# Reordering the steps of a software-pipelined cross-attention on three engines

## The reference

```
q = LN(x) @ Wq + bq          # 32 x 128
k = ctx @ Wk + bk            # 257 x 128
v = ctx @ Wv + bv            # 257 x 128
p = softmax(mask(q k^T / sqrt(8)))   # per head, 32 x 257
x = x + concat(p v) @ Wo + bo
```

## Time and profile before

| | |
|---|---|
| runs | 2421.90, 2426.17, 2428.85 us; median 2426.17 |
| profiled execution: its own time | 2426.17 us |
| its span | 2424.0 us, 55879 instructions |
| TensorE, VectorE, ScalarE, GpSimd busy | 83%, 75%, 60%, 37% |

### The profile page before, as it was taken

The page is one execution under the profiler, slowest core; times in us unless marked ns, Lnnn a source line. Parts: engine busy times, 40 slices in busy tenths (PEclk is TensorE's granted clock), DMA queues, the critical chain, the costliest instruction groups (busy, mean ns, idle before and its releaser), DMA issues. The chain is left out here.

```text
span 2424.0 us, 55879 instructions
## 1 busy us (share of the span) xinstructions
PE 2014.7 (83%) x15622; PEld 1559.9 (64%) x15622; DVE 1811.6 (75%) x5679; ACT 1444.7 (60%) x3917; POOL 905.8 (37%) x1342
## 2 busy tenths in 40 slices
PE   3799999999999999994250168999999989859997
PEld 2588888888888888872140036777777756526665
DVE  5788888888888888864757646888888878754554
ACT  3455555555555555555254537888888878745443
POOL 2433333333333333321124503333333347534554
PEclk8799999999999999996575578999999999969999
DMA  4211111111111011100000012222222200010001
GB/s 134 63 32 31 30 30 30 30 30 30 30 30 28 23 27 28 30 3 1 0 0 0 0 30 65 69 65 66 69 69 68 58 2 1 1 26 1 1 0 35
DMA packets 113672, 77.03 MB, mean 32 GB/s; under 512 B 12384, under 2 KB 99776, under 8 KB 113472
## 3 DMA queue, kind: packets, MB, share of 16 engines
q1 hardware_dynamic: 112086, 73.99, 11.4%
q10 hardware_dynamic: 1194, 1.58, 0.2%
q0 software_dynamic: 320, 0.60, 0.1%
HBM read 71.67 MB, written 4.46 MB: 31 GB/s over the span
## 5 line engine op out<-in xcount | busy, mean ns | idle before, releaser
L758 ACT ACTIVATE a_prob<-a_neg,a_nmax 128x289 f32<-128x289 f32 x512 | 269.9, 529 | 173.7 <-DVE a_nmax L684 171.8
L650 POOL TENSOR_TENSOR a_xn<-a_z,g 128x256 f32<-128x256 f32 x128 | 93.1, 727 | 585.9 <-DVE a_z L714 585.9
L803 PE MATMUL a_score<-a_xnT,a_qT 128*128 128x290 f32 x1536 | 274.2, 314 | 33.7 <-DVE a_qT L738 32.8
L1639 ACT ACTIVATE b_prob<-b_neg,b_nmax 128x257 f32<-128x257 f32 x512 | 255.2, 500 | 70.7 <-DVE b_nmax L1586 70.6
L803 PEld LDWEIGHTS a_score<-a_xnT,a_qT 128*128 128x128 f32 x1536 | 215.6, 190 | 85.6 <-issue 76.9
L830 PE MATMUL a_out<-a_probT,a_xn 128*128 128x256 f32 x1024 | 269.5, 386 | 0.3 <-DVE a_probT L699 0.3
L729 DVE TENSOR_SCALAR a_prob<-a_prob,a_rinv 128x256 f32<-128x256 f32 x512 | 256.9, 561 | 4.5
L684 DVE CUSTOM_DVE_ANT_0 a_neg<-a_score,a_bias 128x289 f32<-128x289 f32 x512 | 216.7, 454 | 40.4 <-PE a_score L803 36.4
L1586 DVE CUSTOM_DVE_ANT_0 b_neg<-b_score,b_bias 128x257 f32<-128x257 f32 x512 | 195.9, 421 | 50.5 <-PE b_score L1682 48.1
L830 PEld LDWEIGHTS a_out<-a_probT,a_xn 128*128 128x128 f32 x1024 | 175.6, 190 | 20.8 <-DVE a_probT L699 2.3
L1560 POOL TENSOR_TENSOR b_last_part<-b_v_rows,b_prob 128x128 f32<-128x128 f32 x128 | 52.0, 406 | 317.4 <-ACT b_prob L1639 317.4
(11 more groups left out here) (472 smaller groups left out, 5273.5 us busy)
## 6 DMA issues: line engine op xcount, KB each, us to landing
a_raw<-in_ctx SPq DMA_DIRECT2D x128, 128.0 KB, 3.2
b_raw<-in_ctx SPq DMA_DIRECT2D x128, 128.0 KB, 3.2
a_kept<-keep SPq DMA_DIRECT2D x32, 257.0 KB, 3.8
b_kept<-keep SPq DMA_DIRECT2D x32, 257.0 KB, 3.6
b_v_rows<-ctx_tail_values SPq DMA_DIRECT2D x32, 256.0 KB, 3.5
a_tail<-latents_normalised SPq DMA_DIRECT2D x64, 64.0 KB
latents_normalised<-lat_affine SPq DMA_DIRECT2D x8, 256.0 KB, 2.3
out<-x SPq DMA_DIRECT2D x1, 2048.0 KB
```

What stands on the lines that cost most here:

```text
L758: nc.scalar.activation(prob[:, par, grp, :], neg[:, grp, :], ACT.Exp, bias=nmax[:, par, grp:grp + 1], scale=-1.0, accum_out=rsum[:, par, g ...
L803: last = nc.tensor.matmul(score_ps[grp % 2][:, 0:even(KEYS0)], qT[:, a, un, bn, 4 * grp:4 * grp + 4, :], xnT[:, c, n, :], start=(p == 0), ...
L1639: nc.scalar.activation(prob[:, n, grp, :], neg[:, par, grp, :], ACT.Exp, bias=nmax[:, par, grp:grp + 1], scale=-1.0, accum_out=rsum[:, n, ...
```

## The change

The lists of VectorE, ScalarE and TensorE in `xattn1` are put in another order. No instruction is added, removed or resized.

| engine | order in a step before | order in a step after |
|---|---|---|
| TensorE | turns(s), weight(s) and raw(s+4), score(s+2), k and v(s+3), projection, last_part(s), values(s) | score(s+2), turns(s), weight(s) and raw(s+4), projection, last_part(s), k and v(s+3), values(s) |
| VectorE | probT(s), reciprocal(s+1), once per tile: sum or x, masks 0 and 1(s+2), kT(s+3), masks 2 and 3(s+2), own(s) | mask 0(s+2), probT(s), masks 1 to 3(s+2), reciprocal(s+1), kT(s+3), own(s), once per tile: x or sum |
| ScalarE | probT(s), turned_in(s+4), exp 0 and 1(s+2), v(s+3), exp 2 and 3(s+2), oT | exp 0(s+2), probT(s), turned_in(s+4), exp 1 to 3(s+2), oT, v(s+3) |

The sum of a tile moves from the start of the next tile's first step to the end of its own last step, and the addition to `x` from the third step of the next tile to the end of its second; VectorE's tail is one step shorter. The wait of `own` for the sum goes, since the sum now stands ahead of it in the same list.

```diff
--- before.py
+++ after.py
@@ -1589,46 +1589,43 @@
 
                 def step(g, j):
                     s, t, u, b = g * 8 + j, tile_of(g, j), j // 4, j % 4
+                    if live(g, j, 2):
+                        mask(g, j, 0)
                     if live(g, j, 0):
                         dve.wait_ge(turned[0], s + 1)
                         nc.vector.tensor_copy(probT[:, 0, :], turn_ps[0][:]).then_inc(probT_ready[0], 1)
+                    if live(g, j, 2):
+                        for grp in range(1, GROUPS):
+                            mask(g, j, grp)
                     if live(g, j, 1):
                         n = (j + 1) % 4
                         dve.wait_ge(exped, s * 4 + 8)
                         wait(dve, weight_ready, s - 2)
                         nc.vector.reciprocal(rinv[:, n, :], rsum[:, n, :]).then_inc(rinv_ready, 1)
-                    if b == 0 and live(g, j, -1):
-                        dve.wait_ge(own_ready, s)
-                        wait(dve, oT_ready, t - 1)
-                        nc.vector.tensor_reduce(oT_sum[:], own[:].rearrange("p b h l -> p b l h"), AX.X, ALU.add).then_inc(sum_ready, 1)
-                    if b == 2 and live(g, j, -4):
+                    if live(g, j, 3):
+                        n = (j + 3) % 4
+                        dve.wait_ge(k_done, s + 4)
+                        dve.wait_ge(kept_loaded[(j + 3) // 4 % 2], (g + (j + 3) // 8 + 1) * 16)
+                        nc.vector.scalar_tensor_tensor(kT[:, n, :], turn_ps[0][:, 0:N_CTX], k.bk1, kept[:, (j + 3) // 4 % 2, n, :],
+                                                       ALU.add, ALU.mult).then_inc(k_ready, 1)
+                    if live(g, j, 0):
+                        dve.wait_ge(out_ready, s + 1)
+                        dve.wait_ge(in_copied, s + 5)
+                        nc.vector.tensor_tensor(own[:, b].rearrange("p h l -> p (h l)"), out_ps[:, 0:P], turned_in[:, (j + 4) % 8, W0:W0 + P],
+                                                ALU.mult).then_inc(own_ready, 1)
+                    if b == 1 and live(g, j, -4):
                         dve.wait_ge(biased, t)
                         dve.wait_ge(proj_ready, t)
                         xt = k.x[:, ds((t - 1) * D, D)]
                         nc.vector.tensor_tensor(xt, proj_ps, xt, ALU.add).then_inc(x_added, 1)
                         wait_apart(k, dve, x_added, t)
                         tile_stats(k, t - 1).then_inc(x_stats_ready, 1)
-                    if live(g, j, 2):
-                        mask(g, j, 0)
-                        mask(g, j, 1)
-                    if live(g, j, 3):
-                        n = (j + 3) % 4
-                        dve.wait_ge(k_done, s + 4)
-                        dve.wait_ge(kept_loaded[(j + 3) // 4 % 2], (g + (j + 3) // 8 + 1) * 16)
-                        nc.vector.scalar_tensor_tensor(kT[:, n, :], turn_ps[0][:, 0:N_CTX], k.bk1, kept[:, (j + 3) // 4 % 2, n, :],
-                                                       ALU.add, ALU.mult).then_inc(k_ready, 1)
-                    if live(g, j, 2):
-                        mask(g, j, 2)
-                        mask(g, j, 3)
-                    if live(g, j, 0):
-                        dve.wait_ge(out_ready, s + 1)
-                        dve.wait_ge(in_copied, s + 5)
-                        if b == 0:
-                            wait(dve, sum_ready, t)
-                        nc.vector.tensor_tensor(own[:, b].rearrange("p h l -> p (h l)"), out_ps[:, 0:P], turned_in[:, (j + 4) % 8, W0:W0 + P],
-                                                ALU.mult).then_inc(own_ready, 1)
-
-                run_steps(dve, step, LEAD, LAG + 1)
+                    if b == 3 and live(g, j, 0):
+                        dve.wait_ge(own_ready, s + 1)
+                        wait(dve, oT_ready, t)
+                        nc.vector.tensor_reduce(oT_sum[:], own[:].rearrange("p b h l -> p b l h"), AX.X, ALU.add).then_inc(sum_ready, 1)
+
+                run_steps(dve, step, LEAD, LAG)
                 dve.wait_ge(x_stats_ready, TILES)
 
             @block.scalar
@@ -1641,6 +1638,11 @@
 
                 def step(g, j):
                     s, t, u, b = g * 8 + j, tile_of(g, j), j // 4, j % 4
+                    if live(g, j, 2):
+
+                        wait(act, last_ready, s - 1)
+                        wait(act, rinv_ready, s - 1)
+                        exp(g, j, 0)
                     if live(g, j, 0):
                         act.wait_ge(turned[1], s + 1)
                         nc.scalar.activation(probT[:, 1, :], turn_ps[1][:], ACT.Copy).then_inc(probT_ready[1], 1)
@@ -1650,22 +1652,16 @@
                         act.wait_ge(in_turned, s + 5)
                         nc.scalar.activation(turned_in[:, (j + 4) % 8, first:end], in_ps[:, first:end], ACT.Copy).then_inc(in_copied, 1)
                     if live(g, j, 2):
-
-                        wait(act, last_ready, s - 1)
-                        wait(act, rinv_ready, s - 1)
-                        exp(g, j, 0)
-                        exp(g, j, 1)
+                        for grp in range(1, GROUPS):
+                            exp(g, j, grp)
+                    if b == 0 and live(g, j, -1):
+                        act.wait_ge(sum_ready, t)
+                        wait(act, proj_ready, t - 1)
+                        nc.scalar.activation(oT[:], oT_sum[:], ACT.Identity, bias=k.bv1).then_inc(oT_ready, 1)
                     if live(g, j, 3):
                         act.wait_ge(v_done, s + 4)
                         nc.scalar.activation(v[:, (j + 3) % 8], turn_ps[1][:, 0:2 * P].rearrange("p (t d) -> p t d", d=D), ACT.Copy)\
                             .then_inc(v_ready, 1)
-                    if live(g, j, 2):
-                        exp(g, j, 2)
-                        exp(g, j, 3)
-                    if b == 0 and live(g, j, -1):
-                        act.wait_ge(sum_ready, t)
-                        wait(act, proj_ready, t - 1)
-                        nc.scalar.activation(oT[:], oT_sum[:], ACT.Identity, bias=k.bv1).then_inc(oT_ready, 1)
 
                 run_steps(act, step, LEAD, LAG)
 
@@ -1700,6 +1696,8 @@
                 def step(g, j):
                     s, t, u, b = g * 8 + j, tile_of(g, j), j // 4, j % 4
                     here, ahead = live(g, j, 0), live(g, j, 4)
+                    if live(g, j, 2):
+                        score(g, j)
                     if here:
                         pe.wait_ge(exped, s * 4 + 4)
                         pe.wait_ge(k_ready, upto(g, s, 3))
@@ -1717,8 +1715,18 @@
                             for kt in range(2):
                                 last = nc.tensor.transpose(in_ps[:, C0 + kt * P:C0 + (kt + 1) * P], raw[:, n, kt, :], k.ident[:])
                         last.then_inc(in_turned, 1)
-                    if live(g, j, 2):
-                        score(g, j)
+                    if here:
+                        wait(pe, own_ready, s)
+                    if b == 1 and live(g, j, -4):
+                        pe.wait_ge(oT_ready, t)
+                        nc.tensor.matmul(proj_ps, oT[:], k.wo1[:], start=True, stop=True, skip_group_check=True).then_inc(proj_ready, 1)
+                    if here:
+                        if b == 2 and live(g, j, -4):
+                            pe.wait_ge(x_added, t)
+                        pe.wait_ge(last_ready, s + 1)
+
+                        nc.tensor.matmul(out_ps[:, 0:P], last_part[:, j % 2], k.ident[:], is_transpose=True, start=True, stop=False,
+                                         skip_group_check=True)
                     if live(g, j, 3):
                         n = (j + 3) % 8
                         pe.wait_ge(in_copied, s + 4)
@@ -1736,17 +1744,6 @@
                                                     start=True, stop=True)
                         last.then_inc(v_done, 1)
                     if here:
-                        wait(pe, own_ready, s)
-                    if b == 1 and live(g, j, -4):
-                        pe.wait_ge(oT_ready, t)
-                        nc.tensor.matmul(proj_ps, oT[:], k.wo1[:], start=True, stop=True, skip_group_check=True).then_inc(proj_ready, 1)
-                    if here:
-                        if b == 2 and live(g, j, -4):
-                            pe.wait_ge(x_added, t)
-                        pe.wait_ge(last_ready, s + 1)
-
-                        nc.tensor.matmul(out_ps[:, 0:P], last_part[:, j % 2], k.ident[:], is_transpose=True, start=True, stop=False,
-                                         skip_group_check=True)
                         values(g, j, 0)
                         values(g, j, 1).then_inc(out_ready, 1)
```

## The result

The changed kernel takes 2447.07 us (median of four runs, 2445.12 to 2448.89) against 2426.22 before: 1.0088 times, 95% interval 1.0069 to 1.0105, or 21 us slower. The forecast was 2441, slower, with 2420 to 2455 as range.

The account below looks back on a forecast made before the run. TensorE's own sum was taken to bound an ordinary step. Four steps of 3.73 plus 0.47, 0.20 and 0.34 made 3.98 us a batch against 3.85, +16 us on 2426.2, less rounding: 2441, range 2420 to 2455.

Parts of the forecast that it names:

- The bound and the loop: Ordinary xattn1 step: TensorE's loop, including a 0.08 wait for the probT copy, takes 3.73 us against 3.76 before.
- TensorE's readiness for the keys: TensorE could start the key projection 2.00 us after the score load, but the probT copy holds it until 2.08.
- The loop through kT: Loop of kT, score, turns, copy, masks and kT through VectorE and TensorE: 3.68 us, just under TensorE's 3.73.
- Sum over heads: Once per tile on VectorE, the reduction behind own delays mask 0 and the probT copy of the next step: +0.47 us.
- x and statistics: Once per tile on VectorE, x and its statistics behind own run into the next step: +0.20 us.
- Projection and oT: Once per tile: v 0.2 late behind oT on ScalarE, projection matmuls 0.22 on TensorE, less 0.08 slack: +0.34 us.
- The tile change: TensorE going straight from values to scores changes tile shape; taken at the 0.20 idle of the values' present exit.
- The sum: Four steps of 3.73 plus 0.47, 0.20 and 0.34 give 3.98 us a batch against 3.85, +16 us over 125 batches.
- Less a little for rounding: Whole kernel: 2426.2 + 16, lowered a little for latencies rounded up, gives 2441 us.
- Faster, TensorE stays the bound: Rival, chance 0.15: key projection starts at 2.00 and scores never wait for kT; 2387 to 2412 us.
- No change: Rival, chance 0.22: once-per-tile work hides half, or handovers are 0.1 per step shorter; 2420 to 2433 us.

Follow-up runs that it names:

- e10: e3 with VectorE's reciprocal moved from ahead of kT to behind it; 2415.62 us, ratio 0.9960 to the kernel before.
- e3: Changed kernel with the edits of both e1 and e2; 2414.15 us, ratio 0.9953 to the kernel before.
- e2: Changed kernel with the sum over heads moved ahead of own in the next tile's first step, and oT behind ScalarE's copy of v; 2426.38 us, ratio 1.0001.
- e1: Changed kernel with only the statistics of x moved from the second step of a tile to the third, before own; 2437.03 us, ratio 1.0046.
- e11: Changed kernel with one edit, ScalarE's oT behind its copy of v; 2443.68 us, ratio 1.0080 to the kernel before.
- e4: Changed kernel with last_part put back between the value projection and the values on TensorE; 2468.38 us, ratio 1.0175 to the kernel before.
- e5: e3 with the two probT copies swapped: ScalarE copies the first bank, VectorE the second; 2412.81 us, ratio 0.9947 to the kernel before.

## Why the forecast was right, and where its sizes were off

- *The bound and the loop.* Right in the main: the `probT` copies hang on mask 0, and TensorE on the copies. The ordinary step came at 3.77 for 3.73, each of its handovers within 0.04. Two terms were wrong without harm to that sum. TensorE's readiness for the keys, 2.00, still held the 0.17 of the change of shape that was said to be out of it; by the trace it is 1.90, and the wait 0.20 and not 0.08. And ScalarE's copy, "ready by 2.54" for a value projection at 2.62, was held against the matmul; its weights are loaded ahead of it, at 2.55, and that load does wait (0.15 of idle time in the fourth step). The loop through kT, forecast at 3.68, under TensorE's 3.73, is not the bound: kT ends 0.24 ahead of the next score in the changed kernel, and e10 shows it for e3.
- *Sum over heads.* 0.47 forecast; the first step takes 4.33, 0.56 over the ordinary one, and e2 takes it all away. The term was too small because `own` starts 0.81 after the values' load (1611.39 to 1612.20), not the 0.71 of the earlier trace rows; the reduction took 1.09, but mask 0 starts 1.01 after it did (1612.52 to 1613.53), as laid out. The prediction also let the reduction cost nothing in the kernel before; there the first step takes 3.93, 0.17 over an ordinary one, with mask 0 behind the reduction and 0.20 late.
- *x and statistics.* 0.20 forecast, 0.42 measured (4.19 - 3.77), and e1 shows it. This is the term that was mis-sized most, by 0.22. Of that 0.09 is the late `own` again. For the rest, I let them overlap at each start; in the trace x starts 0.33 after `own`, the statistics 0.54 after x, and mask 0 only when they are done. (`wait_apart`, between x and the statistics, is one wait and one count by its code, not two of each.)
- *Projection and oT.* 0.34 forecast, 0.13 measured. I counted 0.2 for oT and 0.14 for the projection. e11 puts 0.12 on oT, and only 0.01 is left for the projection. The wait that it stands in is 0.20 and not 0.08, and after the wait the keys' weights are not loaded under running matmuls: from the first matmul of the keys to the first of the values it took 0.44 in that step (1602.44 to 1602.88) and 0.51 in the fourth (1610.33 to 1610.84).
- *The tile change.* The values' exit at 0.57 (0.58 measured) was the right row to take.
- *The sum.* 1.01 was forecast over the four ordinary steps of a tile, 1.14 measured (16.22 - 4 x 3.77), on a step 0.04 longer: 4.05 a batch in the steady part for 3.98. Over 127 steps the stage grew by 23.0 us, not by 16. "Less a little for rounding", which made 2441 of 2442, went the wrong way. That 2441 came within 6 us of 2447 is in part luck: x and its statistics were 0.22 a tile too low and the projection with oT 0.21 too high. Each is worth some 7 us over the 32 tiles; with the second put right and the first not, the forecast would have been 2434.
- *The rivals.* "Faster, TensorE stays the bound" needed the key projection at 2.00; it was at 2.10 in the best step and 2.50 in the third. e3 does get below the kernel before, but not in this rival's way: three moves, two on VectorE and one on ScalarE, separate 21 us slower from 12 us faster, and the key projection stands at 2.10 there too. "No change" rested on half the once-per-tile work hiding; VectorE's part did not hide at all, the projection's did.

What is open: whether the fourth semaphore of e4 is the whole of its extra 0.15, what the second copy's wait costs by itself, and how far e5 could go with that wait gone too.

## What to carry to other kernels

When a reordering makes one engine wait in a loop that had slack before, look for the work that happens only once in several steps: its cost was small in a slack place (0.17 of a reduction of 1.05) and is paid in full in a tight one (0.56, what the idle time of VectorE did not cover). Lay out the new step with handovers from rows, and put rare work where its engine waits for something anyway, here between kT and `own`. When one wait has been found, look for others that end at the same time: here two engines passed on the delay side by side, and an edit to one of them showed almost nothing. With the rare work moved the new order gains 12 us; as written it lost 21, because the sum, the statistics and oT stood in the one place that all engines hang on.

## What the runs showed of the hardware that was not expected

- The idle time that the profile calls "issue" was, at L1738, the wait for the `probT` copy: it was 0.56 in the step where the copy was 0.4 late, 0.17 in an ordinary one, and 0.07 in e5, which the view no longer lists.
- A load with four semaphores to wait for came 0.22 after the last event, one with three 0.07 after it (e4 and the changed kernel): another matmul ahead in the list can carry a wait that has long been met.
- Two matmuls of 0.22 together cost 0.01 when they stood in a wait of 0.20 of the weight loader (e11); the same two cost 0.22 in the kernel before, where nothing waited.
